# A new order of the parts in the second half of an attention and feed-forward layer, with the moments' two passes apart and turned quarters counted by slot

## The chip, the cores and the metric

The kernel runs on one core of one Trainium2 chip. The metric is the device time of one execution in microseconds (us). Each engine of the core has its own queue of instructions and works through it strictly in order: PE multiplies matrices, DVE and ACT work on vectors, POOL helps them, and SP issues the transfers (DMA). The engines meet only at semaphores: an instruction may wait until a counter has reached a value.

## The reference, cut to what matters

2048 rows x of 2048 numbers pass through a layer in fp32:

```python
h = layernorm(x)
# attention: rat_read -> q, k, v, rope, causal softmax -> attn_out
h = rat_write(h, attn_out)            # gates from attn_out, A = exp(-delta * softplus(...))
g_in, u_in = rat_read(h)              # 4 numbers per head -> 2 x 512, each normalised
mlp_out = silu(g_in @ W0) * (u_in @ W1)        # 512 -> 2048 (ctx_1024 holds W0 and W1)
h = rat_write(h, mlp_out)             # again with 632 outputs from 2048
x = x + h
z = layernorm(x)                      # feed-forward: 8 experts of rank 16
scores = 8 * softmax(z @ Wr + br)
x = x + 2 * sum_e scores_e * (z @ A_e) @ B_e
```

`rat_write` scales the state h (512 heads x 4) by A, adds a term from its second input, and does that by several passes over 2048 numbers per row.

## The kernel before, in words

The rows are cut into 16 tiles of 128 (T = 2048, `NT` = 16) and 4 blocks of 4 tiles. A first half projects q, k and v and does the attention; the change does not touch it. The second half, called the mix, is what the change is about. It begins at about 648 us of the profiled span.

The mix is made of parts. A part is named by a letter, a tile (or block) and a name, as `("a", 5, "gates", None)`:

- a (attention write, tile i): `loado`, `load`, `wod` (16 matmuls into two banks), `low`, `delta`, `gates`, `scale`, `sum`, then four quarters `turn` 0 to 3 (PE transposes 512 columns of the state) and `read` 0 to 3 (PE multiplies a turned quarter), `stats`, `norm`.
- m (the MLP, block b, steps 0 to 63): steps 0 to 31 are "up" steps of 12 matmuls, after which ACT takes a silu and DVE multiplies into `m_hT`; steps 32 to 63 are "down" steps of 8 matmul instructions each. t (block b, k of 8): a quarter of the MLP's input is turned by PE, scaled by DVE into one of two buffers `m_raw`, split by ACT into `m_yhi` and by POOL into `m_ylo`.
- w (MLP write, tile i): `load`, `low`, `delta`, `loadx`, `gates`, `scale`, `sum`, `x` (adds x, DVE, one pass over 2048 numbers).
- e (experts, tile i): `stats` (mean and variance: two ACT passes over 2048 numbers, then POOL), `turn` 0 to 3, `down` 0 to 3, `router`, `weigh`, `lowT`, `out` 0 to 3, `store`. s is one part (16 matmuls) that sums a weight table.

What a part does on an engine stands in `write_pe`, `write_dve`, `write_act`, `expert_pe`, `expert_dve`, `expert_act`, `turn_*` and `mlp_*`. The queue of every engine is made by one walk over one list, `order` (line 1113): every part has a number, its place, and the list is sorted by it. A step of the MLP has the place 64 * block + step, so places are in steps; the other parts stand between steps by a base of their tile plus an offset (tables `A_AT`, `W_AT`, `E_AT`, `FIRST_AT`, `A_BASE`, `W_BASE`, `E_BASE`). Since each engine follows the same list, a part that comes early in it is ahead on all engines.

Most small results go through a ring of two PSUM banks (6 and 7): each `turn`, `low`, `delta`, `lowT`, `out` of an expert and both halves of `wod` from tile 4 on take the next bank of the ring in the list's order, and PE waits until the reader of the bank two claims ago has emptied it. A turned quarter is copied by ACT (`keep_quarter`, line 1573, instruction in line 1577) into one of two slots `m_turned`; a slot is free when the `read` or `down` of the quarter before last has been done. This is counted by one semaphore, `quarter_used`, over all quarters.

Lines of the profile that the prediction speaks of: PE L1262 `turn`, L1277 `wod`, L1292 `delta`, L1320 `down`, L1327 `lowT`, L1332 `out`, L1340 the s part, L1349 t, L1362 up steps, L1374 down steps. DVE L1411 the copy of `wod`'s second bank, L1421 to L1434 `gates`, L1442 to L1452 `scale`, L1455 to L1464 `sum`, L1469 `x`, L1514 `weigh`, L1521 `out`, L1531 t, L1545 the product into `m_hT`. ACT L1577 copy of a quarter, L1611 and L1614 `scale`, L1639 and L1643 the two passes of `stats`, L1664 t, L1676 silu. POOL L1717 t. All transfers are issued in line 141.

## Time and profile before

| what | us |
|---|---|
| median of 3 runs | 1874.23 (1872.31 to 1878.28) |
| the profiled execution's own time | 1873.91 |
| its span | 1872.1 |
| PE busy in the span | 1646.7 (88%) |
| DVE, ACT, POOL busy | 1107.7, 872.0, 272.5 |
| waits of PE longer than 0.25 us between 975 and 1780 us | 78.1 in 42 pieces |

PE is the engine that sets the time; it has work in all stretches. How much it could win is read from three things: its idle time before an instruction and what ended it (in square brackets in a timeline, or summed as waits), its granted clock (PEclk, a share of the full 2.4 GHz, so that a stretch with 0.95 had a tenth of its time at 1.2 GHz), and the same two for the engine that it waited for. Idle time of the other engines costs nothing in itself.

### The profile page before, as it was taken

What the parts mean: (1) busy time and instruction counts of PE and PEld (TensorE: products, weight loads), DVE (VectorE), ACT (ScalarE), POOL (GpSimd) and SP (SyncE); (2) the same over time, 40 slices, a digit from 0 to 9 for tenths busy, and PEclk for the clock granted to TensorE, in tenths of its full rate; (3) what the DMA queues carried; (4) which work ended last, traced back from release to release, by engine and by line L of the source; (5) the groups of instructions that cost most, each with busy time, mean ns of one, the idle gap of its engine ahead of it and who ended that gap; (6) DMA issues with size and microseconds to landing.
All of it is one profiled execution on the core that took longest, in us unless ns stands there. A gap on an engine that the chain in (4) does not pass through costs nothing.

```text
span 1872.1 us, 23561 instructions
## 1 busy us (share of the span) xinstructions
PE 1646.7 (88%) x8854; PEld 1139.9 (61%) x8854; DVE 1107.7 (59%) x1729; ACT 872.0 (47%) x1598; POOL 272.5 (15%) x259
## 2 busy tenths in 40 slices
PE   5799999999999856998989899898998998999966
PEld 4565655666666535776657666556676565776544
DVE  6678755888888566353363744645537443454466
ACT  1333236888877544553243544325445334442243
POOL 0235432434320000200011000003000002000000
PEclk7899999999999975899999999998999999999988
DMA  7366568887864343465556555554655544655621
GB/s 299 115 262 250 201 174 237 224 227 218 227 181 114 124 175 120 161 221 186 182 201 211 176 199 202 164 193 132 225 202 185 184 151 153 212 188 172 234 102 68
DMA packets 117221, 348.69 MB, mean 186 GB/s; under 512 B 16226, under 2 KB 33250, under 8 KB 101876
## 3 DMA queue, kind: packets, MB, share of 16 engines
q1 hardware_dynamic: 117108, 347.19, 57.2%
q8 instruction: 70, 1.15, 0.2%
...
## 4 chain that ended last, share of the span: by engine, by line
PE 61%; DVE 22%; ACT 9%; issue 5%; DMA 1%; POOL 1%; SPq 0%; DVEq 0%; ACTq 0%
PE ps L1362 13%; PE ps L1374 10%; PE ps L395 6%; PE ps L819 4%; PE ps L806 4%; PE ps L1277 4%; PE ps L842 4%; PE ps L1320 3%; PE ps L1305 3%; PE ps L1262 3%; ACT a_p L921 3%; PE ps L1332 2%; DVE m_A L1460 2%; DVE m_A L1456 2%; PE ps L368 2%
## 5 line engine op out<-in xcount | busy, mean ns | idle before, releaser
L1362 PE MATMUL ps<-m_yhi,m_win 128*128 128x512 f32 x1024 | 357.9, 417 | 8.7 <-ACT m_raw L1676 8.7
L1374 PE MATMUL ps<-m_wod,m_hT 128*128 128x512 f32 (+1 forms) x1024 | 303.1, 444 | 8.0 <-DVE m_hT L1545 8.0
L1374 PEld LDWEIGHTS ps<-m_wod,m_hT 128*128 128x128 f32 x1024 | 169.5, 196 | 146.8 <-issue 146.4
L1362 PEld LDWEIGHTS ps<-m_yhi,m_win 128*128 128x128 f32 x1024 | 198.1, 193 | 60.8 <-issue 16.0
L863 DVE TENSOR_REDUCE a_negmax<-ps 128x1 f32<-128x640 f32 (+7 forms) x176 | 180.8, 1027 | 60.5 <-PE ps L809 59.6
L1362 PE MATMUL ps<-m_ylo,m_win 128*128 128x512 f32 x512 | 206.1, 403 | 0.0
L921 ACT ACTIVATE a_p<-ps,a_negmax 128x128 f32<-128x128 f32 (+7 forms) x256 | 188.5, 750 | 28.6 <-DVE a_negmax L863 26.1
L819 PE MATMUL ps<-ident,a_p 128*128 128x128 f32 x1152 | 157.8, 276 | 1.3 <-DVE a_pT L876 1.2
L1545 DVE TENSOR_TENSOR m_hT<-m_raw,ps 128x512 f32<-128x512 f32 x64 | 43.5, 684 | 172.5 <-PE ps L1362 159.6
L1577 ACT ACTIVATE m_turned<-ps 128x512 f32<-128x512 f32 x128 | 74.1, 591 | 152.5 <-PE ps L1262 152.4
L806 PE MATMUL ps<-a_k,a_q 128*128 128x512 f32 (+3 forms) x384 | 124.0, 402 | 16.6 <-ACT a_p L921 14.8
L819 PEld LDWEIGHTS ps<-ident,a_p 128*128 128x128 f32 x1152 | 124.0, 142 | 3.2 <-DVE a_pT L876 1.9
L1362 PEld LDWEIGHTS ps<-m_ylo,m_win 128*128 128x128 f32 x512 | 99.4, 194 | 24.8 <-issue 4.9
L395 PE MATMUL ps<-p_yT,p_wqkv 128*128 128x512 f32 x256 | 112.3, 593 | 0.0
L1262 PE MATMUL ps<-ident,m_hs 128*128 128x128 f32 x464 | 75.5, 296 | 38.8 <-DVE m_hs L1464 14.1
L876 DVE COPY a_pT<-ps 128x512 f32<-128x512 f32 (+3 forms) x190 | 108.1, 576 | 1.3 <-PE ps L819 0.7
L1705 POOL TENSOR_TENSOR m_scale<-m_scale,mhalf 128x2 f32<-128x2 f32 x16 | 12.4, 772 | 634.5 <-DVE m_scale L1482 634.5
L935 ACT ACTIVATE a_pT<-ps 128x512 f32<-128x512 f32 (+3 forms) x154 | 83.9, 545 | 34.8 <-PE ps L819 34.6
L806 PEld LDWEIGHTS ps<-a_k,a_q 128*128 128x128 f32 x384 | 63.3, 192 | 54.8 <-ACT a_p L921 31.5
L1320 PE MATMUL ps<-e_A,m_turned 128*128 128x136 f32 x512 | 76.1, 295 | 21.7 <-ACT m_turned L1577 21.6
L1262 PEld LDWEIGHTS ps<-ident,m_hs 128*128 128x128 f32 x464 | 60.1, 155 | 49.9 <-DVE m_hs L1464 15.3
L1521 DVE TENSOR_TENSOR m_hs<-ps,m_hs 128x512 f32<-128x512 f32 x56 | 38.2, 687 | 88.0 <-PE ps L1332 87.8
...
## 6 DMA issues: line engine op xcount, KB each, us to landing
m_win<-mlp_in_split SPq DMA_DIRECT2D x128, 512.0 KB, 4.2
m_wod<-in_wod2T SPq DMA_DIRECT2D x128, 316.0 KB, 3.1
...
p_xT<-in_xT SPq DMA_DIRECT2D x16, 1024.0 KB, 8.9
p_x<-in_x SPq DMA_DIRECT2D x16, 1024.0 KB, 10.3
...
a_k<-qk_split SPq DMA_DIRECT2D x128, 128.0 KB, 7.3
...
```

Of the source, the lines that this page charges most:

```text
L395: m = nc.tensor.matmul(ps[:, b, :], wq[:, k, col:col + P], yT[:, k, :], start=(ic == 0), stop=(ic == HCH - 1))
L806: nc.tensor.matmul(ps[:, bank + at, c0:c0 + kn], qs[s][:, qt * P:qt * P + P], ks[s][:, k0:k0 + kn], start=True, stop=k0 + kn < klen)
L819: m = nc.tensor.transpose(ps[:, b, P * m_:P * m_ + P], src[:, j, P * k:P * k + P], ident[:, :])
L842: m = nc.tensor.matmul(ps[32 * hh:32 * hh + 32, 6, c0:P * qn], a_v[s][:, k, HD * hh:HD * hh + HD], kept[:, hh, k, c0:P * qn], start=(k == ...
L863: V.tensor_reduce(negmax[:, n % 4, 0:len(units[n][3])], by_head(n, score_banks(n)), AX_X, ALU.max, negate=True).then_inc(max_ready, 1)
L876: V.tensor_copy(kept[:, heads[j0]:heads[j1] + 1, k0:k1 + 1, P * q:P * q + P], ps[:, b, 0:P * len(part)].rearrange("p (a k b) -> p a k b", ...
L921: m = S.activation(dst[:, j, :], src[:, j, :], ACT.Exp, bias=negmax[:, n % 4, j:j + 1], accum_out=rsum[:, si % 2, q * 4 + hh:q * 4 + hh + 1])
L935: S.activation(kept[:, heads[j0]:heads[j1] + 1, k0:k1 + 1, P * q:P * q + P], ps[:, b, 0:P * len(part)].rearrange("p (a k b) -> p a k b", a ...
L1262: m = nc.tensor.transpose(bank_of(what, i, "turn", q)[:, P * j:P * j + P], h[:, P * (4 * q + j):P * (4 * q + j) + P], ident[:, :])
L1320: m = nc.tensor.matmul(bank_of("e", i, "down")[:, 0:EW + NE], tT[quarter["e", i, q] % 2][:, P * (j % 4):P * (j % 4) + P], wA[:, j, :], sta ...
L1362: m = nc.tensor.matmul(bank_of("m", blk, step), win[s][:, wl, ic, :], y[:, k, :], start=(ic == 0 and p3 == 0), stop=(ic == HCH - 1 and p3 ...
L1374: m = nc.tensor.matmul(ps[:, b, 0:cn], hT[:, k, P * q:P * q + P], w2[s][:, c0:c0 + cn], start=(k == 0), stop=(k == MCH - 1))
```

## The change

The tables of places are replaced by one dictionary `PLACES`, with other numbers; the construction of `order` from it is the same. `stats` of the experts becomes two parts: `mean` (first ACT pass and the small scaling, with a new semaphore `emean_ready`) and `spread` (second ACT pass, and POOL). `quarter_used` becomes two semaphores, one for each slot, so that the copy of quarter n waits for the uses of its own slot alone. The instructions are the same in number and kind.

```diff
+PLACES = {'A': {'loado': -2,
+       'wod': 0,
...
+ 'W': {'load': -3.18, 'low': 0, 'delta': 1.6, 'loadx': 2, 'gates': 2.66, 'scale': 3.59, 'sum': 5.81, 'x': 6.93},
...
-        W_AT = [("load", None, -3), ("low", None, 0), ("delta", None, 1.6), ("loadx", None, 2), ("gates", None, 4),
-                ("scale", None, 5), ("sum", None, 6), ("x", None, 8)]
...
-        placed = [(40, ("s", 0, "sum", None))]
+        placed = [(PLACES["s"], ("s", 0, "sum", None))]
...
-        hs_scaled, skip_ready, hs_ready, turnq_mm, quarter_used = (
+        quarter_used = sems("quarter_used", 2)
...
+        emean_ready = sem("emean_ready")
...
+        def wait_for_quarter(e, what, i, q):
+
+            n = quarter[what, i, q]
+            e.wait_ge(quarter_used[n % 2], n // 2 + 1)
...
             n = quarter[what, i, q]
             act.wait_ge(turnq_mm, n + 1)
-            act.wait_ge(quarter_used, n - 1)
+            act.wait_ge(quarter_used[n % 2], n // 2)
...
-            if part == "stats":
-
-                X, m, spare = hs[hs_of["w", i]], e_mv[i % 4], m_x[x_place(i)]
+
+            X, m, spare = hs[hs_of["w", i]], e_mv[i % 4], m_x[x_place(i)]
+            if part == "mean":
                 act.wait_ge(x2_ready, i + 1)
                 act.wait_ge(elw_ready, i - 3)
                 n = act_own.then_inc(S.activation(spare[:, :], X[:, :], ACT.Identity, accum_out=m[:, 0:1]))
                 act.wait_ge(act_own.sem, n)
-                n = act_own.then_inc(S.activation(m[:, 2:3], m[:, 0:1], ACT.Identity, scale=-1.0 / D))
-                act.wait_ge(act_own.sem, n)
+                S.activation(m[:, 2:3], m[:, 0:1], ACT.Identity, scale=-1.0 / D).then_inc(emean_ready, 1)
+            if part == "spread":
+                act.wait_ge(emean_ready, i + 1)
                 S.activation(spare[:, :], X[:, :], ACT.Square, bias=m[:, 2:3],
                              accum_out=m[:, 1:2]).then_inc(evar_ready, 1)
```

The offsets of all parts, before and after, in steps (a part of tile i stands at its base plus this):

| | before | after |
|---|---|---|
| a, tiles 4 to 15: load, gates, scale, sum | 4.2, 6, 7, 8 | 5.27, 7.93, 8.57, 9.57 |
| a: turn 0 to 3 | 12, 12.5, 14, 15 | 13.57, 14.07, 15.57, 16.57 |
| a: read 0 to 3, stats, norm | 13.5, 14.5, 15.5, 16.5, 17.5, 19 | 15.07, 16.07, 17.79, 18.07, 19.07, 20.57 |
| a, tiles 0 to 3: from wod to turn 0, to read 0 | 6, 7 | 6.52, 7.57 |
| w: gates, scale, sum, x | 4, 5, 6, 8 | 2.66, 3.59, 5.81, 6.93 |
| e: stats, or mean and spread | 8.5 | 8.68 and 12.99 |
| e: turn 2, turn 3, down 2, down 3 | 12.5, 13.5, 14, 15 | 14.61, 14.62, 15.47, 15.48 |
| e: out 0 to 3 | 20, 20.5, 21.5, 22 | 19.1, 20.5, 20.51, 22.57 |
| t of block 1, first and last | 55.5, 62.5 | 57.05, 59.87 |
| t of block 2, first and last | 119.5, 126.5 | 120.21, 128.83 |
| t of block 3, first and last | 183.5, 190.5 | 185.58, 191.64 |
| s | 40 | 30.75 |

The bases stay within 0.7 of a step, but for that of tile 2 in w and e (81.01 for 80).

On PE, at the start of the mix, the rows before are the turn of tile 0's first quarter (`m_hs_161`, L1262) and tile 2's `wod` (`m_first_oT_203`, L1277), of which the first matmuls are shown:

```order
L1292 MATMUL ps<-m_duT_144,m_lowT_148 128x512
L1262 MATMUL ps<-ident,m_hs_161 128x128 x4
L1277 MATMUL ps<-m_wod_135,m_first_oT_203 128x512
L1277 MATMUL ps<-m_wod_135,m_first_oT_203 128x120
L1277 MATMUL ps<-m_wod_137,m_first_oT_203 128x512
```

After, with the lines of the changed file (L1361 is `turn`, L1376 `wod`, L1391 `delta`):

```order
L1391 MATMUL ps<-m_duT_144,m_lowT_148 128x512
L1376 MATMUL ps<-m_wod_135,m_first_oT_203 128x512
L1376 MATMUL ps<-m_wod_135,m_first_oT_203 128x120
L1376 MATMUL ps<-m_wod_137,m_first_oT_203 128x512
L1376 MATMUL ps<-m_wod_137,m_first_oT_203 128x120
L1376 MATMUL ps<-m_wod_129,m_first_oT_203 128x512
L1376 MATMUL ps<-m_wod_129,m_first_oT_203 128x120
L1376 MATMUL ps<-m_wod_131,m_first_oT_203 128x512
L1376 MATMUL ps<-m_wod_131,m_first_oT_203 128x120
L1361 MATMUL ps<-ident,m_hs_161 128x128 x8
```

Tile 2's `wod` has moved ahead of tile 0's turns, and two quarters are turned in a row. The same holds for tile 3 and tile 1.

On DVE, at the end of block 0's up steps, the rows before are tile 6's `sum` (`m_hs_161` and `m_A_165`) between the last two products into `m_hT`:

```order
L1545 TENSOR_TENSOR m_hT<-m_raw_188,ps 128x512
L1486 SCALAR_TENSOR_TENSOR m_scale<-m_moments,m_scale 128x2
L1455 TENSOR_TENSOR m_hs_161<-m_hs_161,m_A_165 128x512x3
L1456 SCALAR_TENSOR_TENSOR m_A_165<-m_A_165,m_gate_179 128x1536
L1460 TENSOR_TENSOR m_A_165<-m_A_165,m_att_out 128x1536
L1464 TENSOR_TENSOR m_hs_161<-m_hs_161,m_A_165 128x512x3
L1545 TENSOR_TENSOR m_hT<-m_raw_189,ps 128x512
```

After (L1644 is the product, L1554 to L1563 `sum`, L1541 to L1551 `scale`, L1625 the copy of the s part):

```order
L1541 TENSOR_TENSOR m_tmp_177<-m_delta_175,m_att_ab 128x512
L1545 TENSOR_TENSOR m_tmp_177<-m_tmp_177,m_att_out 128x512
L1551 TENSOR_TENSOR m_hs_161<-m_hs_161,m_tmp_177 128x512
L1625 COPY e_Asum<-ps 128x136
L1644 TENSOR_TENSOR m_hT<-m_raw_189,ps 128x512
L1585 SCALAR_TENSOR_TENSOR m_scale<-m_moments,m_scale 128x2
L1554 TENSOR_TENSOR m_hs_161<-m_hs_161,m_A_165 128x512x3
L1555 SCALAR_TENSOR_TENSOR m_A_165<-m_A_165,m_gate_179 128x1536
```

The last product now stands ahead of the `sum`, and the s part comes just before it.

On ACT, in block 1, the rows before are the two passes of tile 1's `stats` (`m_hs_163`), a silu pair with its table loads, `scale` of tile 9 (`m_hs_161`, `m_A_165`), and the copies of tile 1's turned quarters:

```order
L1639 ACTIVATE m_x,e_moments_153<-m_hs_163 128x2048
L1641 ACTIVATE e_moments_153<-e_moments_153 128x1
L1643 ACTIVATE m_x,e_moments_153<-m_hs_163,e_moments_153 128x2048
L1676 ACT_TABLE_LOAD
L1676 ACTIVATE m_raw_188<-ps 128x512
L1676 ACTIVATE m_raw_189<-ps 128x512
L1678 ACT_TABLE_LOAD
L1611 ACTIVATE m_hs_161<-m_hs_161,nmr_52,rstd_51 128x2048
L1614 ACTIVATE m_A_165<-m_A_165 128x1536
L1577 ACTIVATE m_turned_186<-ps 128x512
L1577 ACTIVATE m_turned_187<-ps 128x512
```

After (L1738 is `mean`, L1743 `spread`, L1776 silu, L1676 the copies, L1710 and L1713 `scale`):

```order
L1738 ACTIVATE m_x,e_moments_153<-m_hs_163 128x2048
L1740 ACTIVATE e_moments_153<-e_moments_153 128x1
L1776 ACT_TABLE_LOAD
L1776 ACTIVATE m_raw_188<-ps 128x512
L1776 ACTIVATE m_raw_189<-ps 128x512
L1778 ACT_TABLE_LOAD
L1676 ACTIVATE m_turned_186<-ps 128x512
L1676 ACTIVATE m_turned_187<-ps 128x512
L1710 ACTIVATE m_hs_161<-m_hs_161,nmr_52,rstd_51 128x2048
L1713 ACTIVATE m_A_165<-m_A_165 128x1536
L1743 ACTIVATE m_x,e_moments_153<-m_hs_163,e_moments_153 128x2048
```

The second pass has moved behind the first two copies, and `scale` of the other tile too.

## Rows read from the trace of the kernel before

**Rows 1.** Part 6 of the page: the loads of x in the mix.

```profile
m_x<-in_x SPq DMA_DIRECT2D x14, 1024.0 KB, 5.5
```

**Rows 2.** Windows: us, PE, PEld, DVE, ACT, POOL busy (x), granted clock, DMA, GB/s.

```profile
975.00:1265.00 290.00, 257.78 (x1172) 181.96 (x1173) 150.77 (x217) 123.10 (x192) 17.49 (x19) 0.95 0.56 187
1265.00:1550.00 285.00, 252.92 (x1153) 179.78 (x1152) 151.28 (x217) 122.48 (x187) 19.93 (x20) 0.95 0.54 181
1550.00:1780.00 230.00, 212.33 (x920) 148.94 (x918) 100.78 (x139) 86.76 (x132) 14.27 (x16) 0.98 0.58 191
```

**Rows 3.** Waits of PE, 975 to 1780 us: us in total, times, longest.

```profile
PE ps L1332 <- DVE m_hs L1521: 22.2, 8, 3.5
PE ps L1320 <- ACT m_turned L1577: 16.1, 6, 2.8
PE ps L1262 <- ACT m_turned L1577: 11.1, 3, 3.9
PE ps L1349 <- DVE m_raw L1531: 10.5, 5, 4.9
PE ps L1362 <- ACT m_raw L1676: 8.7, 6, 2.1
PE ps L1277 <- ACT e_lowT L1655: 4.0, 7, 0.6
PE ps L1262 <- DVE m_hs L1469: 3.2, 3, 2.2
```

**Rows 4.** Timeline of PE at tile 0's first turn.

```profile
676.38 1.12 PE L1262 MATMUL ps<-ident,m_hs 128*128 128x128 f32 x4 [5.86 <-DVE m_hs L1464]
677.28 6.11 PE L1277 MATMUL ps<-m_wod,m_first_oT 128*128 128x512 f32 x16
```

**Rows 5.** Waits of DVE, 648 to 750 us, as rows 3.

```profile
DVE m_mlp_ab L1411 <- PE ps L1277: 20.0, 4, 12.4
DVE m_hs L1452 <- ACT m_hs L1611: 8.0, 3, 3.7
```

**Rows 6.** Timeline around block 0's first down step, and the s part.

```profile
885.78 1.19 PE L1374 MATMUL ps<-m_wod,m_hT 128*128 128x512 f32 x1 [7.97 <-DVE m_hT L1545]
...
915.22 3.88 PE L1340 MATMUL ps<-e_A,e_weighted 128*128 128x136 f32 x32
```

**Rows 7.** Groups of DVE: count, busy us, mean ns, idle before.

```profile
L1464 DVE TENSOR_TENSOR m_hs<-m_hs,m_A 128x1536 f32<-128x1536 f32 x26 | 45.7, 1758 | 0.9
```

**Rows 8.** Timeline of tile 1's third `out`, and the window behind it, as rows 2.

```profile
1111.06 2.07 PE L1332 MATMUL ps<-e_B,e_lowT 128*128 128x512 f32 x2 [2.77 <-DVE m_hs L1521]
...
1111.00:1116.40 5.40, 5.34 (x15) 3.66 (x16) 3.23 (x7) 2.65 (x5) 0.20 (x1) 0.72 0.06 22
```

**Rows 9.** Timeline: the second pass of tile 1's `stats`, and its first `down`.

```profile
1053.60 2.01 ACT L1643 ACTIVATE m_x<-m_hs,e_moments 128x2048 f32<-128x2048 f32 x1
...
1063.40 2.18 PE L1320 MATMUL ps<-e_A,m_turned 128*128 128x136 f32 x8 [2.61 <-ACT m_turned L1577]
```

**Rows 10.** POOL's line 1717 (ns: shortest, median, longest), and a timeline in block 1.

```profile
L1717 POOL TENSOR_TENSOR m_ylo<-m_raw,m_yhi x32: 1255/1274/3722, 752.9 to 1579.2; 128x512 fp32r<-128x512 f32 x32
...
982.37 3.72 POOL L1717 TENSOR_TENSOR m_ylo<-m_raw,m_yhi 128x512 fp32r<-128x512 f32 x1 [2.87 <-ACT m_yhi L1664]
...
984.99 2.72 DVE L1460 TENSOR_TENSOR m_A<-m_A,m_att_out 128x1536 f32<-128x1536 f32 x1
```

**Rows 11.** The chain of waits: one up step, from its start, with its us.

```profile
1141.46 2.81 PE ps L1362 x12
```

**Rows 12.** Timeline of the end; its second row is four down steps.

```profile
1759.31 0.69 DVE L1521 TENSOR_TENSOR m_hs<-ps,m_hs 128x512 f32<-128x512 f32 x1 [5.88 <-PE ps L1332]
...
1766.01 8.81 PE L1374 MATMUL ps<-m_wod,m_hT 128*128 128x512 f32 x32
...
1782.75 1.97 PE L1262 MATMUL ps<-ident,m_hs 128*128 128x128 f32 x8 [7.93 <-DVE m_hs L1469]
...
1830.95 0.48 PE L1327 MATMUL ps<-ident,e_weighted 128*128 128x128 f32 x1 [16.79 <-DVE e_weighted L1514]
```

More of the change, by code:

```diff
@@ L1079, in program @@
         CONSTS_SET, LOWS_SET, ONES_SET = ZEROS + 8, ZEROS + 12, ZEROS + 13
-        A_AT = [("loado", None, -2), ("wod", None, 0), ("low", None, 2), ("delta", None, 4), ("load", None, 4.2),
-                ("gates", None, 6), ("scale", None, 7), ("sum", None, 8), ("turn", 0, 12), ("turn", 1, 12.5),
-                ("read", 0, 13.5), ("turn", 2, 14), ("read", 1, 14.5), ("turn", 3, 15), ("read", 2, 15.5),
-                ("read", 3, 16.5), ("stats", None, 17.5), ("norm", None, 19)]
-        W_AT = [("load", None, -3), ("low", None, 0), ("delta", None, 1.6), ("loadx", None, 2), ("gates", None, 4),
-                ("scale", None, 5), ("sum", None, 6), ("x", None, 8)]
@@ L1091, in program @@
-        E_AT = [("stats", None, 8.5), ("turn", 0, 10), ("turn", 1, 10.5), ("down", 0, 12), ("turn", 2, 12.5),
-                ("down", 1, 13), ("turn", 3, 13.5), ("down", 2, 14), ("down", 3, 15), ("router", None, 16),
-                ("weigh", None, 17.2), ("lowT", None, 18.5), ("out", 0, 20), ("out", 1, 20.5), ("out", 2, 21.5),
-                ("out", 3, 22), ("store", None, 23)]
-        FIRST_AT = [("loado", None, -100), ("load", None, -99.9), ("wod", None, 0), ("low", None, 1),
-                    ("delta", None, 2), ("gates", None, 3), ("scale", None, 4), ("sum", None, 5), ("turn", 0, 6),
-                    ("turn", 1, 6.5), ("read", 0, 7), ("turn", 2, 7), ("read", 1, 7.5), ("turn", 3, 7.5),
-                    ("read", 2, 8), ("read", 3, 8.5), ("stats", None, 9), ("norm", None, 10)]
@@ L1106, in program @@
         for i in range(NT):
[L1107 to L1112 removed]
+            for what, table, base in (("a", "FIRST" if i < TB else "A", "a"), ("w", "W", "w"), ("e", "E", "e")):
+                for part, at in PLACES[table].items():
+                    q = int(part[-1]) if part[-1].isdigit() else None
+                    placed.append((PLACES[base][i] + at, (what, i, part.rstrip("0123"), q)))
@@ L1307, in write_pe @@
                                          read2[:, jj, :, :].rearrange("p b c -> p (b c)"), start=True, stop=True)
-                m.then_inc(quarter_used, 1)
+                m.then_inc(quarter_used[quarter[what, i, q] % 2], 1)
         def expert_pe(i, part, q):
@@ L1322, in expert_pe @@
                                          start=(j == 0), stop=(j == DCH - 1))
-                m.then_inc(quarter_used, 1)
+                m.then_inc(quarter_used[quarter["e", i, q] % 2], 1)
             if part == "lowT":
@@ L1473, in write_dve @@
                     yv = bank_of(what, i, "read", a).rearrange("p (j o h) -> p j o h", o=RD2, h=HPC)
-                    dve.wait_ge(quarter_used, quarter[what, i, 2 * a + 1] + 1)
+                    wait_for_quarter(dve, what, i, 2 * a + 1)
                     for o in range(RD2):
@@ L1492, in expert_dve @@
             if part == "router":
-                dve.wait_ge(quarter_used, quarter["e", i, 3] + 1)
+                wait_for_quarter(dve, "e", i, 3)
                 dve.wait_ge(evar_ready, i + 1)
@@ L1707, in expert_pool @@
         def expert_pool(i, part, q):
-            if part == "stats":
+            if part == "spread":
                 m = e_mv[i % 4]
```

119 lines of the change are left out of this document (107 added, 12 removed).

## The prediction

> **What bounds the kernel now.** I read the page first: PE is busy in 88% of the span. Then the windows of the mix: in the two long stretches from 975 to 1265 and from 1265 to 1550 us PE is busy 258 of 290 and 253 of 285 us, at a mean granted clock of 0.95 [rows 2]. So PE bounds them, and what can be won is what it stands still and what it does at 1.2 instead of 2.4 GHz. Last I read who ended PE's waits. From 975 to 1780 us seven groups of them make 75.8 us [rows 3], and they repeat with each tile, since each tile's parts stand at the same offsets. The reader is to see there that no engine is full: DVE is busy 151 of 290 us [rows 2], and PE waits for it because of what stands ahead in DVE's queue, not because of how much there is. The same goes for ACT. A new order can therefore pay, with not one instruction less.
>
> **The change part by part.** Durations are of the profiled execution, which took 1873.9 us (span 1872.1); the median of the three runs is 1874.2, so the two can be taken as one.
>
> (a) Tiles 0 to 3. PE waits 5.86 us for tile 0's `sum` and only then does tile 2's `wod`, 6.11 us [rows 4]; DVE in turn waits for that `wod`. After the change `wod` stands ahead of the turn, so it fills PE's wait. DVE's waits for `wod` in this stretch are 20.0 us, of which 12.4 are the very first and stay: 7.6 go. DVE also waits 8.0 us for ACT's scaled state [rows 5]; ACT does that pass after three copies of quarters and in future after two, and it starts sooner because the copies do: I take 5 of 8.0. The bounds are nothing, if ACT becomes what DVE waits for, and 7.6 + 8.0 = 15.6; I take 12.6, nearer to the upper one, since DVE's waits for `wod` are sure to go. The weights of the earlier `wod` are loaded two tiles ahead in SP's queue, and the store of the state that SP issues at the turn now stands behind them, which helps them.
>
> (b) The end of block 0's up steps. PE waits 7.97 us for the last product [rows 6], which DVE does after tile 6's `sum`; four passes of 1.76 us stand ahead of it [rows 7], 7.0 us. They move behind it, and about 1 us is left. The s part, 3.88 us of PE [rows 6], goes from step 40 to just ahead of this place; it fills part of what would remain in any case, so it isn't counted. With 1 us of clock that such a wait costs: 8 us. Bounds: 0 and 7.97 + 3.88 = 11.9.
>
> (c) The turned quarters of the MLP's input (t) and the experts' first turns between them. PE waits 10.5 us for DVE's `m_raw` and 11.1 us for ACT's copies [rows 3], in three blocks. The cause is a second moments pass of 2.01 us [rows 9] and the `scale` and `sum` of another tile between them. In the new order the mean stands before the first t, the spread behind most, and in block 1 all eight t come before tile 8's `sum`; in block 2 the `sum` of tile 12 still stands before the fifth t. I lay out what is left as 2 to 3 us per block, 7 in all: 14.6 us won. Bounds 0 and 21.6.
>
> (d) The tile cycles of blocks 1 to 3. `out` 2 waits 22.2 us in eight places [rows 3] because its ring bank is that of `out` 1, and DVE adds `out` 1 after the `gates` and the `stats` of two other tiles. `gates` now stand before or right behind `out` 0, and `out` 1 and 2 come together, on the bank before: these waits go. `down` 0 waits 16.1 us and the silu pairs make PE wait 8.7 us; both stand behind the two passes of `stats`, and the one pass of 2.01 us that moves [rows 9], together with `x` standing one step earlier, is enough for waits of at most 2.8 and 2.1 us [rows 3]. The wait for `x` at the experts' first turn (3.2) goes too, since `gates` of w stand 1.3 steps earlier. Sum 22.2 + 16.1 + 8.7 + 3.2 = 50.2. What comes in its place: `wod` waits 4.0 us in seven places now, for one ACT copy [rows 3]. In the new order it follows `lowT` and, in tiles 10 and perhaps 14, `w` `delta` at once on PE; it then waits for ACT's copy of a quarter, then for two passes over `delta`: I set 2.7 us, just under the longest ACT wait of its kind, 2.8. With 0.9 in the five others that is 9.9, so 6 more. `out` 0 and 1, and `low` behind them, can wait fractions of a microsecond: for these and for what I do not see I set 12 tile cycles at 0.6, the size of the small waits in rows 3: 7. Won: 50.2 - 6 - 7 = 37. Bounds: 0 and 50.2.
>
> The SP queue: `load` of a stands 1.1 steps later, `x` 1.1 steps earlier with `loadx` where it was. Five steps lie between `loadx` and `x`, of 8.81 / 4 = 2.2 us at least [rows 12], 11 us; the transfer takes 5.5 [rows 1]. That hides it; if it didn't, DVE would wait at each of 16 `x`. The two `quarter_used` semaphores only loosen a wait, and the split of `stats` adds one wait on ACT for its own earlier instruction: nothing.
>
> (e) The clock. After a wait of 2.77 us the granted clock was 0.72 in the next 5.4 us [rows 8], that is 0.28 x 5.4 = 1.5 us lost. Over the stretches 0.05 x 290, 0.05 x 285 and 0.02 x 230 make 33 us [rows 2], an upper bound, since time in which PE stands still is in it. Seven long `out` waits, six `down` waits and some four of (c) times 1.5 are 25. The new waits of (d) take some of that back, about a third: I take 16. Bounds 0 and 25.
>
> (f) The end. The first turn of tile 12 waits 7.93 us for `x` [rows 12]; DVE's `gates` of w 12 stand behind `out` 0 of tile 11, for which DVE waits 5.88 us [rows 12]. `gates` move ahead of it: 5 us. The wait of 16.79 us [rows 12] stays, since DVE is busy there from one end to the other with `gates`, `scale` and `sum` of tiles 14 and 15, and with the same passes after the change. The last tile's first copies come one pass of 2 us sooner, and `x` of tile 15 a little: 3. Won 8; bounds 0 and 13.
>
> Sum: 12.6 + 8 + 14.6 + 37 + 16 + 8 = 96.2; 1873.9 - 96.2 = 1777.7, so 1778. All upper bounds together: 15.6 + 11.9 + 21.6 + 50.2 + 25 + 13 = 137.3, 1737.
>
> **A rule weighed.** POOL's `m_ylo` passes take 1.27 us in the median, but up to 3.72 beside a pass of DVE's `sum`, which itself takes 2.72 instead of 1.76 [rows 7, 10]. The Trainium skill ("SBUF — State Buffer", section "SBUF: two separate sides") says that DVE and GpSimd take turns on a shared pair of ports, which is "an exclusive lock, not a bandwidth split": a DVE pass with two SBUF inputs shuts a GpSimd one out. This case's trace agrees with that place; by the rule the closer t of block 1, with `gates` and `scale` of tile 8 between them, would be slow ones. What that would make of the time is the second rival.
>
> **The rivals.**
> 1. The waits move instead of going: with one in-order queue per engine, what no longer stands ahead of `out` stands ahead of something else. For it: the new gaps that I find already (`wod` behind `delta`, t 5 of block 2 behind a `sum`). Against it: DVE and ACT have half of their time free [rows 2]. It halves (c), (d) and (e): 1778 + (14.6 + 37 + 16)/2 = 1812.
> 2. POOL paces the t of blocks 1 and 3. Eight passes at 3.72 are 29.8 us [rows 10]; PE has some three down steps of 2.2 us and 5 us of turns and `down` between the first and last t of block 1, 12 in all, and six steps and 5 us, 18, in block 3 [rows 12]. It would wait 18 + 12 = 30 more: 1808. Against it: half of all 32 passes took at most 1.27.
> 3. Slower than before: `x` of w now follows its `sum` almost at once, and `sum` comes before the `norm` of a, the last product of a pair and, in two tiles, `out` 3. If PE needs one of these before DVE is through, it waits for four passes, 7.0 us [rows 7], and 1.5 for the clock [rows 8], in each of 12 cycles: 12 x 8.5 = 102, so 1778 + 102 = 1880. It decides against the change from a mean wait of 6.5 us per cycle on. Against it: PE does four up steps of 2.81 us, 11 us, until it needs the bank of a product [rows 11].
> 4. The order changes but the time does not: something that the waits hide, such as the weights' transfers, sets the pace. Then 1874. Against it: in rows 3 no wait of PE was ended by a transfer.
>
> **How the numbers follow.** The forecast, 1778, gets 0.63 (its own range 1756 to 1800); rival 1, at 1812, 0.20; rival 2, at 1808, 0.08; rival 3, 0.05; rival 4, 0.04. The range for 8 times in 10: below, not quite all upper bounds, 1748; above, rival 1 with another quarter of its waits kept, 1836. A change of 0.3% (5.6 us) is what a measurement of this kernel tells from none: faster 0.91, the same 0.04, slower 0.05.
>
> **What would show it.** In the profile after, L1332's wait for DVE and L1320's for ACT are near nothing in blocks 1 to 3; the down steps of block 0 start with at most 1 to 2 us of wait; the stretch of tiles 0 to 3 is some 12 us shorter; the clock in blocks 1 and 2 is 0.98; `wod` has its longest wait in tile 10; the 16.8 us before tile 13's `lowT` are still there. I am wrong if the waits of PE between blocks 1 and 3 sum to over 45 us, if the t have 3 us each, or if `x` waits for a transfer.

## The result, and the profile after

The changed kernel takes 1761.84 us, median of four runs (1759.10 to 1764.08), against 1874.98 us (1872.31 to 1878.28) for the kernel before on the same chip: a ratio of 0.9395, 95% interval 0.9373 to 0.9417, or 113 us less. I had forecast 1778 with a range of 1748 to 1836. The profiled execution took 1764.08 us (span 1762.3).

Every line number of PE's, DVE's and ACT's code is 99 higher than before: L1361 is `turn`, L1376 `wod`, L1419 `down`, L1426 `lowT`, L1431 `out`, L1448 t, L1461 and L1473 up and down steps; on DVE L1554 to L1563 `sum`, L1568 `x`, L1620 `out`, L1630 t; on ACT L1676 the copy of a quarter, L1710 `scale`, L1723 `norm`, L1738 and L1743 `mean` and `spread`. First the windows, columns as in [rows 2], whose three stretches now lie here:

```profile
946.00:1205.00 259.00, 248.09 (x1176) 176.51 (x1174) 158.35 (x220) 123.02 (x193) 34.48 (x20) 0.99 0.60 205
1205.00:1462.00 257.00, 248.61 (x1168) 177.70 (x1169) 155.48 (x218) 121.92 (x188) 32.09 (x20) 0.98 0.62 208
1462.00:1670.00 208.00, 206.13 (x926) 145.87 (x924) 96.94 (x139) 88.16 (x136) 13.09 (x16) 1.00 0.61 199
```

PE is now busy in 248 of 259, 249 of 257 and 206 of 208 us, and at nearly full clock. Its busy time fell too, with the same number of instructions. The whole mix in one window shows how much, before and after:

```profile
648.00:1870.00 1222.00, 1058.56 (x4752) 750.88 (x4752) 620.14 (x881) 506.08 (x784) 79.31 (x80) 0.93 0.53 178
```

```profile
648.00:1870.00 1222.00, 1034.17 (x4752) 737.46 (x4752) 623.39 (x881) 502.89 (x784) 105.34 (x80) 0.96 0.53 179
```

The same 4752 instructions of PE take 1058.6 us before and 1034.2 after: 24.4 us less. Most of it is the clock: of PE's busy time in the mix 122.2 us lie in stretches granted 1.2 GHz before and 81.3 after, and half of the difference, 20.5 us, is what the clock gave back, by an estimate that takes all of PE's work as twice as fast at 2.4 GHz. The other 4 us were not traced. The rest is time in which PE stood still: its waits of 0.2 us and more in the mix, added up from the timeline, are 164.8 us before and 79.3 after, 85.5 less. 24.4 and 85.5 make the 110 us by which the profiled executions differ. The waits of PE from 946 to 1670 us, to be read beside [rows 3]:

```profile
PE ps L1448 <- ACT m_y L1723: 5.1, 2, 3.7
PE ps L1361 <- DVE m_raw L1630: 3.8, 1, 3.8
PE ps L1448 <- DVE m_raw L1630: 2.7, 2, 2.3
PE ps L1376 <- ACT m_turned L1676: 2.0, 2, 1.1
PE ps L1376 <- ACT e_lowT L1755: 1.5, 2, 0.9
PE ps L1376 <- ACT m_delta L1691: 1.4, 1, 1.4
PE ps L1361 <- ACT m_att_out L1686: 1.4, 2, 0.7
PE ps L1376 <- DVE m_hs L1620: 1.0, 1, 1.0
```

The waits for `out` (22.2 us), for the first `down` (16.1) and for the silu pairs (8.7) are not there any more. What is new is small but for two waits of 3.7 and 3.8 us: t of block 2 waits for tile 11's `norm`, and a turn behind it for a t that stands behind tile 12's `sum`.

### The profile page after: what moved, and what is told of

The parts are those of the page before. It is cut to its first block, busy times and chain, and to the rows that moved or that the text cites. A ratio compares the mean times of both kernels' runs of the same rounds, so it can differ in the third digit from the quotient of the medians.

```text
span 1762.3 us, 23558 instructions
## 1 busy us (share of the span) xinstructions
PE 1624.5 (92%) x8854; PEld 1128.2 (64%) x8854; DVE 1111.1 (63%) x1729; ACT 868.9 (49%) x1598; POOL 298.6 (17%) x259
## 3 DMA queue, kind: packets, MB, share of 16 engines
q1 hardware_dynamic: 117108, 347.19, 60.8%
## 4 chain that ended last, share of the span: by engine, by line
PE 75%; DVE 13%; ACT 6%; issue 3%; DMA 1%; POOL 1%; SPq 0%; DVEq 0%; ACTq 0%
PE ps L1461 20%; PE ps L1473 13%; PE ps L509 6%; PE ps L933 5%; PE ps L920 4%; PE ps L956 4%; PE ps L1376 4%; PE ps L1419 3%; PE ps L1361 3%; PE ps L1404 3%; PE ps L1431 3%; ACT a_p L1035 3%; PE ps L482 2%; PE ps L1391 1%; PE ps L495 1%
## 5 line engine op out<-in xcount | busy, mean ns | idle before, releaser
L1461 PE MATMUL ps<-m_yhi,m_win 128*128 128x512 f32 x1024 | 349.0, 409 | 0.0
L1473 PE MATMUL ps<-m_wod,m_hT 128*128 128x512 f32 (+1 forms) x1024 | 298.0, 440 | 1.3 <-DVE m_hT L1644 0.9
L1473 PEld LDWEIGHTS ps<-m_wod,m_hT 128*128 128x128 f32 x1024 | 166.7, 194 | 136.6 <-issue 136.5
L1461 PEld LDWEIGHTS ps<-m_yhi,m_win 128*128 128x128 f32 x1024 | 193.6, 189 | 47.8 <-issue 4.1
L1461 PE MATMUL ps<-m_ylo,m_win 128*128 128x512 f32 x512 | 202.9, 396 | 0.0
L1644 DVE TENSOR_TENSOR m_hT<-m_raw,ps 128x512 f32<-128x512 f32 x64 | 43.7, 684 | 172.9 <-PE ps L1461 164.8
L1676 ACT ACTIVATE m_turned<-ps 128x512 f32<-128x512 f32 x128 | 72.7, 593 | 146.9 <-PE ps L1361 139.8
L1805 POOL TENSOR_TENSOR m_scale<-m_scale,mhalf 128x2 f32<-128x2 f32 x16 | 21.7, 1358 | 534.9 <-DVE m_scale L1581 534.9
L1461 PEld LDWEIGHTS ps<-m_ylo,m_win 128*128 128x128 f32 x512 | 97.0, 189 | 23.7 <-issue 4.1
L1049 ACT ACTIVATE a_pT<-ps 128x512 f32<-128x512 f32 (+3 forms) x154 | 83.9, 545 | 34.1 <-PE ps L933 34.0
L920 PEld LDWEIGHTS ps<-a_k,a_q 128*128 128x128 f32 x384 | 63.4, 192 | 55.1 <-ACT a_p L1035 32.0
L509 PEld LDWEIGHTS ps<-p_yT,p_wqkv 128*128 128x128 f32 x256 | 47.6, 190 | 55.0 <-issue 55.0
L1361 PE MATMUL ps<-ident,m_hs 128*128 128x128 f32 x464 | 68.7, 284 | 13.1 <-DVE m_raw L1630 3.8
L482 PEld LDWEIGHTS ps<-p_read,p_xT 128*128 128x128 f32 x512 | 68.0, 215 | 19.0 <-issue 19.0
L669 ACT ACTIVATE p_y<-p_z,p_yscale 128x512 f32<-128x512 f32 x48 | 35.6, 804 | 89.9 <-DVE p_yscale L588 89.9
```

Source lines behind the costliest of these rows:

```text
L482: m = nc.tensor.matmul(ps[:, j // 4, zw * (j % 4):zw * (j % 4) + zw], p_xT[i % 2][:, j, :], read1[:, j, :, :].rearrange("p a b -> p (a b)" ...
L509: m = nc.tensor.matmul(ps[:, b, :], wq[:, k, col:col + P], yT[:, k, :], start=(ic == 0), stop=(ic == HCH - 1))
L920: nc.tensor.matmul(ps[:, bank + at, c0:c0 + kn], qs[s][:, qt * P:qt * P + P], ks[s][:, k0:k0 + kn], start=True, stop=k0 + kn < klen)
L1049: S.activation(kept[:, heads[j0]:heads[j1] + 1, k0:k1 + 1, P * q:P * q + P], ps[:, b, 0:P * len(part)].rearrange("p (a k b) -> p a k b", a ...
L1361: m = nc.tensor.transpose(bank_of(what, i, "turn", q)[:, P * j:P * j + P], h[:, P * (4 * q + j):P * (4 * q + j) + P], ident[:, :])
L1461: m = nc.tensor.matmul(bank_of("m", blk, step), win[s][:, wl, ic, :], y[:, k, :], start=(ic == 0 and p3 == 0), stop=(ic == HCH - 1 and p3 ...
```

## The experiments

Each kernel has the changed code and differs from the changed kernel (1761.8), or from the kernel of experiment 1, in places alone. All ratios are to the kernel before, which was run again beside each set of experiments (medians of 1874.5 to 1876.2 us), with their 95% intervals. A difference to 1761.8, which comes from another set, can be off by a microsecond or two for that reason.

**1. The code without the places.**

```diff
-'W': {'load': -3.18, ..., 'gates': 2.66, 'scale': 3.59, 'sum': 5.81, 'x': 6.93},
+'W': {'load': -3, ..., 'gates': 4, 'scale': 5, 'sum': 6, 'x': 8},
...
+# A, E, FIRST, the bases, t and s as before as well; spread directly behind mean
```

> The changed code with the places of the kernel before (spread directly behind mean, so each engine has its instructions in the old order). My theory: all of the gain is the order; the two semaphores and the split of stats cost and give nothing, so 1874 within 0.3% (1868 to 1880), and PE's longest waits stand at the old places (7.97 before the first down step, 16.79 before tile 13's lowT). Rival: counting the quarters by slot alone loosens ACT's copies, of whose waits PE had 11.1 us at the turns; then it is 1865 or less.

1875.95 us, ratio 1.0003 (0.9994 to 1.0013). In the old order the two semaphores and the split give nothing, so the gain needs the new places. Whether the new order would do as well with one semaphore for all quarters was not tried.

**2. Tiles 0 to 3 put back.**

```diff
-'FIRST': {..., 'wod': 2.06, 'low': 3.06, ..., 'turn0': 8.58, 'turn1': 8.59, 'turn2': 9.2, ...}
+'FIRST': {..., 'wod': 0, 'low': 1, ..., 'turn0': 6, 'turn1': 6.5, 'turn2': 7, ...}
```

> The changed kernel, but tiles 0 to 3 have the offsets of the kernel before, nothing else. The stretch up to the first t was 103.5 us before and 89.1 after. My theory (term a): all 14.4 of it come back and nothing else moves: 1776, the waits before the first turns of tiles 0 and 1 are back at 5.9 and 4.3 us. Rival: what is lost here is given back later, since block 0's up steps have slack in their other engines: under 1770.

1780.24 us (0.9493, 0.9476 to 0.951), 18.4 more than the change. In the trace the stretch before the first t is 106.2 us long, and everything behind it takes as long as in the changed kernel to within 1 us. That is four more than I expected, and the pair of profiles that I had worked from is why. Seven profiled kernels have the new order of this stretch (the change and experiments 3, 4 and 8 to 11): it takes 83.5, 83.7, 85.4, 85.4, 85.6, 89.1 and 89.2 us, and the 89.1 is the change. Six have the old order: 103.5 to 106.2 us, and the 103.5 of the kernel before is the low end. The means, 105.2 and 86.0, differ by 19.2, which agrees with the 18.4.

**3. The outs put back, with `gates` and `scale` of w.**

```diff
-'W': {..., 'gates': 2.66, 'scale': 3.59, ...}   'E': {..., 'out0': 19.1, 'out1': 20.5, 'out2': 20.51, 'out3': 22.57, ...}
+'W': {..., 'gates': 4, 'scale': 5, ...}         'E': {..., 'out0': 20, 'out1': 20.5, 'out2': 21.5, 'out3': 22, ...}
```

> The changed kernel, but the four outs stand at 20, 20.5, 21.5 and 22 again, and gates and scale of w at 4 and 5. My theory (term d, its out part, and e): the waits of the third out come back, eight of 2.8 to 3.5 us or 22 us of waits, and each of them with 1.5 us of clock: 34 more, 1796; the granted clock from block 1 on goes from 0.99 to 0.97. Rival 1 (waits only move): with the other waits gone DVE's queue has more slack, the out waits that come back are matched by shorter others, and it is under 1774.

1791.68 us (0.9556, 0.9534 to 0.9579): 29.8 more, near the 34 that I expected, but not by the waits that I expected. The edit puts two things back at once, the outs and `gates` and `scale` of w, so that 29.8 is not the price of either. DVE and PE in block 1:

```profile
1138.30 0.68 DVE L1620 TENSOR_TENSOR m_hs<-ps,m_hs 128x512 f32<-128x512 f32 x1
...
1140.73 1.75 DVE L1554 TENSOR_TENSOR m_hs<-m_hs,m_A 128x1536 f32<-128x1536 f32 x1
...
1145.97 1.76 DVE L1563 TENSOR_TENSOR m_hs<-m_hs,m_A 128x1536 f32<-128x1536 f32 x1
1147.65 0.68 DVE L1620 TENSOR_TENSOR m_hs<-ps,m_hs 128x512 f32<-128x512 f32 x1
```

```profile
1148.39 1.22 PE L1431 MATMUL ps<-e_B,e_lowT 128*128 128x512 f32 x1 [6.08 <-DVE m_hs L1620]
```

The third `out` now stands behind another tile's whole `sum` on DVE, since its base had moved as well, and the fourth waits 6.08 us. That is the one long wait before an `out`; another, of 6.53, stands before tile 12's `delta`, the first t of block 3 waits 5.88 instead of 1.37, and the turns at the end wait longer too. Putting back one part of a fitted order can make waits that neither kernel has.

**4. The second moments pass put back.**

```diff
-'E': {'mean': 8.68, ..., 'spread': 12.99, ...}
+'E': {'mean': 8.68, ..., 'spread': 8.69, ...}
```

> The changed kernel, but spread stands directly behind mean (8.69 instead of 12.99). Three answers. As the prediction has it, the pass that moves is what frees the first down (16.1 us of waits) and the silu pairs (8.7), with some nine long waits and 1.5 us of clock each: up to 38 more, 1800. If the earlier x is what does it, the second pass is done before the copies are wanted, and it is within 4 us: under 1766. If both are needed, each first down waits about half of its 2.6 us, too short for the clock to fall, and t of blocks 1 to 3 some 2 us more: 12 more, 1774. I hold the last for likeliest.

1762.57 us (0.9399, 0.9381 to 0.9417): no difference from the change, where I had held 12 us more for likeliest. The new part `spread`, on which my terms for `down` and t rested in part, gains nothing that this measurement can tell. In the trace the turns of blocks 1 and 3 wait 1.4 and 2.0 us for ACT's copies again (3.4 us instead of 0.8), but no `down` of blocks 1 to 3 stands among the waits, and from the first up step on the profiles take 1016.8 and 1016.4 us.

**5 and 6. From the kernel before: `x` alone, then the row of w.**

```diff
 # 5
-'W': {..., 'gates': 4, 'scale': 5, 'sum': 6, 'x': 8}
+'W': {..., 'gates': 4, 'scale': 5, 'sum': 6, 'x': 6.93}
 # 6
-'W': {..., 'gates': 4, 'scale': 5, 'sum': 6, 'x': 8}
+'W': {..., 'gates': 2.66, 'scale': 3.59, 'sum': 5.81, 'x': 6.93}
```

> The places of the kernel before in the changed code, with one number changed: x of w stands at 6.93 instead of 8. DVE then adds x directly behind sum, ahead of the last product of a pair. The run with only spread put back lost nothing, so x may be what freed the first down and the silu pairs. Theory 1, x alone does it: the waits for m_turned at the first down (16.1 us), for m_raw at the silu pairs (8.7) and at the experts' first turn (3.2) go, with some nine falls of the clock of 1.0 to 1.5 us each: 1876 less 28 less 9 is 1839. Theory 2, as the prediction had it, x and the moved pass are needed together: half of the waits and little clock, 1860. Theory 3: DVE is busy there anyway and the product that is now behind x makes PE wait: 1872 or more. I hold the first for likeliest, with 1845.

> The places of the kernel before in the changed code, with the whole row of w as in the change: gates 2.66, scale 3.59, sum 5.81, x 6.93; a, e, t, s and tiles 0 to 3 are as before. gates then stand ahead of the first out. Theory 1: that removes the third out's waits too (22.2 us, with eight falls of the clock of 1.5), on top of what x gives: 1839 less 34 is 1805, 60 to 70% of the whole gain from one row of four numbers. Theory 2 (waits move): gates ahead of out 0 make it wait for out 0 instead and the moments of a still stand between out 0 and 1, so half of it: 1822 or more.

`x` alone: 1871.57 us (0.9976, 0.9967 to 0.9985), 4 us, where I had held 1845 for likeliest. In its trace DVE has `x` of this tile done 9.9 us after it begins the third `out`, against 10.4 in the kernel before: the new place is ahead of one product of 0.68 us and of nothing else. The row of w: 1796.32 us (0.9584, 0.9568 to 0.96), 79.5 us or seven tenths of the whole gain, from four numbers; I had expected 1805. ACT in the `x` kernel, ahead of tile 1's first `down` (lines one lower here: L1775 is silu, L1709 and L1712 `scale`, L1675 the copies):

```profile
1060.17 2.01 ACT L1742 ACTIVATE m_x<-m_hs,e_moments 128x2048 f32<-128x2048 f32 x1
...
1063.58 1.09 ACT L1775 ACTIVATE m_raw<-ps 128x512 f32<-128x512 f32 x2
1064.68 1.28 ACT L1777 ACT_TABLE_LOAD   x1
1065.97 2.10 ACT L1709 ACTIVATE m_hs<-m_hs,nmr,rstd 128x2048 f32<-128x2048 f32 x1
1067.98 1.47 ACT L1712 ACTIVATE m_A<-m_A 128x1536 f32<-128x1536 f32 x1
1069.35 1.06 ACT L1675 ACTIVATE m_turned<-ps 128x512 f32<-128x512 f32 x2
```

This is the cause of the 16.1 us in [rows 3], and I had it wrong: the copies that `down` waits for stand behind the second pass only at several removes; directly ahead of them is `scale` of tile 9, which follows a silu pair, which follows the passes, and the first pass waits for DVE's `x` (6.15 us in this trace). As long as DVE hands over `x` late, the whole chain is late. The kernel with the row of w has the same order on ACT, and the copies' waits there are 6.1 us instead of 16.1 (next experiment).

**7. `gates` alone.**

```diff
-'W': {..., 'gates': 4, ...}
+'W': {..., 'gates': 2.66, ...}
```

> The places of the kernel before in the changed code, with one number changed: gates of w stands at 2.66 instead of 4, so its six instructions are ahead of the first out on DVE. The run with the whole row of w was 79 us faster than before, that with x alone 4. My theory: gates is what does it, since without it the third out waits for nothing and sum comes earlier by the same 3 us: 1796 plus the 4 that x gave, 1800. Rival: scale and sum moved with it (5 to 3.59, 6 to 5.81) carry a good part, and it is 1820 or more.

1833.76 us (0.9778, 0.9757 to 0.9799), 41 us; I expected 75. Waits of PE from 975 to 1700 us:

```profile
PE ps L1418 <- ACT m_turned L1675: 16.1, 6, 2.8
PE ps L1360 <- ACT m_turned L1675: 11.2, 3, 3.9
PE ps L1447 <- DVE m_raw L1629: 10.3, 5, 4.9
PE ps L1460 <- ACT m_raw L1775: 8.4, 6, 2.0
```

The waits for `out` are gone, those for `down` and silu stand as in [rows 3]. With the row of w the same view reads:

```profile
PE ps L1360 <- ACT m_turned L1675: 10.6, 3, 3.9
PE ps L1418 <- ACT m_turned L1675: 6.1, 6, 1.1
PE ps L1375 <- ACT e_lowT L1754: 4.0, 7, 0.6
PE ps L1447 <- DVE m_raw L1629: 3.8, 2, 2.1
PE ps L1447 <- DVE m_hs L1619: 3.0, 2, 2.4
```

So `gates` frees `out`, and the other three numbers, on top of it, free the silu pairs and most of `down`. `x` was worth 4 by itself and some 38 are won by `scale`, `sum` and `x` on top of `gates`; how these 38 divide among the three, and what they give without `gates`, was not tried.

**8. t put back.**

```diff
-'t': [..., 57.05, 57.45, 57.85, 58.26, 58.66, 59.06, 59.47, 59.87, ...]
+'t': [..., 55.5, 56.5, 57.5, 58.5, 59.5, 60.5, 61.5, 62.5, ...]
```

> The changed kernel with the t of blocks 1 to 3 at their old places (55.5, 56.5 and so on). Theory (term c): 10.4 us of waits return, with three or four falls of the clock of 1.5: 1762 and 15 is 1777. Rival: the waits at t came from the moments pass and from x, which now stand elsewhere, so the old places cost under 5 us: 1767 or less.

1783.69 us (0.9507, 0.9491 to 0.9524): 21.9 more, where I expected 15. In its trace PE waits 7.74 us for a t behind tile 8's `sum`, 5.85 and 5.70 for `norm` before the first t of blocks 2 and 3, and 4.56 for the last t of block 2.

**9. The end of block 0's up steps put back.**

```diff
-'s': 30.75
+'s': 40, and tile 6's sum at 30.9
```

> The changed kernel, but tile 6's sum again stands ahead of block 0's last product (at 30.9 instead of 31.57), and s at 40. Theory (term b): the 7.1 us of waiting before the first down step come back, with 1 to 3 us of clock: 1771. Rival: what DVE does late here it gives back in the down steps that follow, or s at its new place mattered by itself: outside 1767 to 1775.

1772.17 us (0.9454, 0.944 to 0.9468): 10.3 more, within the range expected. In its trace the wait before the first down step is 9.90 us, against 0.87 in the change and 7.97 before, so that 9.0 of the 10.3 are the wait.

**10. Three parts alone, in the kernel before.**

```diff
+the row of w, the offsets of tiles 0 to 3, s at 30.75 and tile 6's sum behind the last product
 # all else, t and the outs and the offsets of a included, as before
```

> The places of the kernel before with three parts of the change alone: the row of w, the offsets of tiles 0 to 3, and tile 6's sum behind block 0's last product (with s at 30.75). Theory, the parts add up: 1796.3 - 18.4 - 10.3 = 1767.6, within 6 us of the whole change (1762), although putting t back in the whole change cost 22 and putting the outs back cost 30, since those places only fit each other. Rival: they don't add up, because the t and out places of the change are needed for the gain of the others; then it is 1775 or more.

1767.47 us (0.943, 0.9411 to 0.9449), where the sum of the parts gave 1767.6. These three make 107 of the 113 us. What is then missing, t and the outs with the offsets of a, the bases and `spread`, adds only 6 us, although putting back t alone cost 22: the old places of t do harm only among the new places of the others. The 30 of experiment 3 cannot be set beside these 6, since it took back `gates` and `scale` of w too, which this kernel has.

**11 and 12. The waits that are left.**

```diff
+('a', 11, 'norm'): 118.9, ('a', 15, 'norm'): 182.9      # ahead of x
+('a', 12, 'sum'): 126.38, ('a', 8, 'gates'): 59.1       # behind the sixth t
+('w', 14, 'low'): 255.475, ('w', 14, 'delta'): 256.02, ('w', 15, 'low'): 256.5
+('e', 12, 'lowT'): 258.45, ('e', 13, 'weigh'): 261.7, ('e', 13, 'lowT'): 262.0
+('e', 13, 'turn', 1): 256.03, ('e', 13, 'out', 1 to 3): 265.0 to 265.02, ('e', 15, 'mean'): 270.7
 # 12 has this and
+'s': -0.6
```

> The changed kernel with other places for its remaining waits: norm of tiles 11 and 15 ahead of x (waits of 3.69 and 1.37 us before t of blocks 2 and 3), sum of tile 12 behind the sixth t instead of the fifth's product (3.77), gates of tile 8 behind the sixth t (2.25), and in the end: low and delta of tile 14 right behind the last down step, tile 12's lowT ahead of the second moments pass, tile 13's weigh ahead of tile 14's sum, three of tile 13's outs behind tile 15's x on DVE, tile 15's mean behind two copies. Theory: 3 + 1.4 + 3.8 + 2.2 us of waits in the blocks, with 1.5 us of clock for three of them, and 5 in the end: 20 less, 1742. Rival (waits move): each of these parts now makes something else wait, sum of tile 12 its own turn and the last down step's copy above all, and it is within 5 us of the change: 1757 or more.

> The version with the other places for the remaining waits (1744.8), with the s part moved from step 30.75 to just ahead of block 0's first t, where PE waits 3.85 us for the last norm of the first tiles. s takes 3.9 us at full clock. Where it stands now the clock is full; at its new place the granted clock is 0.50, so that it takes some 7.7 us, of which 3.85 lie in the wait: 3.9 saved in block 0 and 3.9 lost here, 1745, if the clock there stays at 0.50 up to the first up step as before. If the clock follows what PE does, it is granted full sooner, and s and the t behind it (8.1 us of PE at 0.50) win: up to 4 from the t and 2 from s, 1739. I hold 1741 for likeliest: the clock rises with the filler before the t are through. Over 1748 would say that s delays DVE's first products of the t.

The first gives 1744.78 us (0.9298, 0.9277 to 0.9319), 17 us less than the change, near the 20 expected, and the lowest median here. In its trace the 3.69 us before t of block 2 are 0.77, the 3.77 before a turn 0.47, and tile 13's `lowT` waits 5.13 us instead of 12.61, though tile 14's turns and first `down` now wait 6.9 us (the four below) where 2.9 stood:

```profile
1699.73 0.48 PE L1443 MATMUL ps<-ident,e_weighted 128*128 128x128 f32 x1 [5.13 <-DVE e_weighted L1630]
...
1709.45 1.10 PE L1378 MATMUL ps<-ident,m_hs 128*128 128x128 f32 x8 [2.73 <-DVE m_hs L1585]
1712.21 3.99 PE L1436 MATMUL ps<-e_A,m_turned 128*128 128x136 f32 x16 [1.66 <-ACT m_turned L1693]
1716.98 1.11 PE L1378 MATMUL ps<-ident,m_hs 128*128 128x128 f32 x4 [0.78 <-DVE m_last_hs L1637]
1719.78 1.11 PE L1378 MATMUL ps<-ident,m_hs 128*128 128x128 f32 x4 [1.69 <-DVE m_last_hs L1637]
```

With s in front of the first t it is 1747.99 us (five runs, 0.9322, 0.9308 to 0.9335): the same within the intervals, where I had held 1741 for likeliest. The wait there is filled, but s itself, which I had priced at half clock, ran at full:

```profile
730.47 3.97 PE L1456 MATMUL ps<-e_A,e_weighted 128*128 128x136 f32 x32 [1.17 <-DMA e_A<-in_expA]
```

PE starts it when its weights land, 1.17 us into the wait. From the end of s to the first up step it is then 9.4 us; without s it was 13.8 from the start of the wait, of which 3.85 were the wait, so the t themselves won only half a microsecond. What ate at least part of the gain is at the end of the up steps, where s had covered a wait for the last product: 0.87 us before, 2.98 now.

## Why the prediction was right, and where it was not

The mechanism was right: PE sets the time, the gain is waits that one in-order queue made for another, and with them clock. The sum was 96 where 110 came (profiled executions). The waits were forecast at 80 and measured at 85.5, PE's shorter work at 16 and measured at 24.4. The terms that were mis-sized are (d), 9 too low, and (e), 8 too low; (c) and (f) were 4 and 3 too high. That the sum came out nearer than its terms is in part luck. By its steps:

**(a), 12.6 forecast.** The stretch went from 103.5 to 89.1 us, 14.4, and putting it back cost 18.4. Its make-up on DVE was off: DVE's waits for `wod` fell by 4.1 instead of 7.6, those for ACT's `scale` by 6.6 instead of 5 ([rows 5] beside these, DVE, 648 to 735 us). What I had seen in [rows 4] came true: tile 2's `wod` now stands ahead of tile 0's turn, with no wait between (the second fence):

```profile
DVE m_mlp_ab L1510 <- PE ps L1376: 15.9, 2, 12.0
...
DVE m_hs L1551 <- ACT m_hs L1710: 1.4, 2, 1.0
```

```profile
673.14 6.08 PE L1376 MATMUL ps<-m_wod,m_first_oT 128*128 128x512 f32 x16
679.06 1.04 PE L1361 MATMUL ps<-ident,m_hs 128*128 128x128 f32 x8
```

In this pair of profiles the gain is all waits (PE's fell from 39.5 to 25.7 us, its busy time only from 64.1 to 63.4). Over the six and seven profiles of experiment 2 the waits fall by 12.7 us in the mean, which is the term, and PE's busy time by 6.5. The term held no clock, and six of these 6.5 are clock: half of the fall in PE's busy time at 1.2 GHz, from 41.8 to 29.7 us.

**(b), 8.** The wait of 7.97 us is 0.87, 7.1 less; experiment 9 measured 10.3, more than the wait that the kernel before had:

```profile
867.85 2.39 PE L1473 MATMUL ps<-m_wod,m_hT 128*128 128x512 f32 x8 [0.87 <-DVE m_hT L1644]
```

**(c), 14.6.** The lines for t and the turns beside it make 13.2 us after (5.1, 3.8, 2.7 and two of 0.8), against 21.6 in [rows 3], 1.3 for a `norm` and 1.0 for turns behind a t: 10.7 won. The part missed is `norm` of tiles 11 and 15, which is behind `sum` and `x` of w on DVE; I had laid out t against `sum` and not against `norm`:

```profile
1206.15 1.12 PE L1448 MATMUL ps<-ident,m_y 128*128 128x128 f32 x4 [3.69 <-ACT m_y L1723]
...
1231.90 1.33 PE L1361 MATMUL ps<-ident,m_hs 128*128 128x128 f32 x6 [3.77 <-DVE m_raw L1630]
```

The second is the fifth t of block 2 behind tile 12's `sum`, as forecast. Experiment 11 takes both away.

**(d), 37.** 54.2 us of waits (these four groups and `wod`) became 7.9: 46.3. `wod` waits 5.9 where I had set 9.9, and what I did not see is 2.0 where I had set 7; its longest wait is in tile 10, 1.4 instead of 2.7. The term was too low by 9, and one step had the wrong cause: `x` alone does not free `down` (experiment 5), and the moved pass is not needed for it (experiment 4). `gates` of w ahead of the first `out` frees the outs and leaves the 16.1 us of `down` as they were; `scale`, `sum` and `x` moved as well bring them to 6.1 (experiments 6 and 7), and the last 6.1 go with other places of the change, which ones was not tried. For the pass to matter, ACT would have to be late because of it; ACT was late because DVE was.

**(e), 16.** 24.4 us less of PE's busy time, 20.5 of them by the estimate from the clock. They were won where I had looked for them: between block 0's first up step and tile 12's first turn PE's busy time at 1.2 GHz fell from 61.7 to 15.0 us, worth 23, near the bound of 25; in tiles 0 to 3 it stayed (39.1 and 39.3), and at the end it rose. I had let the new waits take a third back. Between 946 and 1670 us they are 1.4 us and less but for three, and behind a wait of that size the clock did not fall; it did behind the longer ones. Windows of the changed kernel behind the wait of 1.38 us, around that of 2.25 and behind that of 3.69, and last of experiment 4's kernel around the same wait as the second:

```profile
1055.00:1062.00 7.00, 6.32 (x29) 4.27 (x30) 0.28 (x1) 2.79 (x7) 0.00 (x0) 1.00 0.47 158
959.40:966.20 6.80, 6.77 (x28) 4.58 (x29) 6.29 (x7) 5.60 (x6) 3.75 (x3) 0.75 0.12 20
1205.40:1212.20 6.80, 6.05 (x17) 3.98 (x18) 0.81 (x1) 3.88 (x7) 1.28 (x1) 0.50 0.97 355
...
956.70:963.50 6.80, 6.69 (x35) 4.54 (x36) 6.29 (x7) 5.54 (x6) 3.68 (x3) 1.00 0.33 102
```

The granted clock is 1.00, 0.75 and 0.50, and 1.00 in the last: a wait of 2.24 us that the clock followed in one kernel's execution and not in the other's. The length of a wait alone does not settle it, so a fixed 1.5 us for each wait could only be near. One profile sizes this term loosely as well: the kernel of experiment 4, as fast as the change, has 14 us less of PE's busy time in the mix and 9 us more of waits. In the sum of the waits (d)'s 9 more and (c)'s 4 less nearly cancel.

**(f), 8.** From the wait before tile 12's first turn to the end it is 92.2 us before (1774.8 to 1867.0) and 86.9 after (1670.3 to 1757.1): 5.3. The turn's wait went from 7.93 to 2.57, as forecast. The wait before tile 13's `lowT` is 12.61, not 16.8, but a new one of 4.03 stands before tile 12's first `out`, whose copy on ACT is behind the second moments pass of tile 13. PE's waits there fell by 8.3 us (34.1 to 25.8), but its own work took 3 us more (57.9 to 60.8 us) for the same number of instructions. The mean clock of the stretch, 0.83 and 0.84, hides why: it counts the time in which PE stands still. Of PE's busy time 13.5 us lie at 1.2 GHz before and 18.9 after, worth 2.7 us.

```profile
1672.82 1.78 PE L1361 MATMUL ps<-ident,m_hs 128*128 128x128 f32 x8 [2.57 <-DVE m_hs L1568]
...
1699.34 1.12 PE L1431 MATMUL ps<-e_B,e_lowT 128*128 128x512 f32 x2 [4.03 <-ACT e_lowT L1755]
...
1721.23 0.48 PE L1426 MATMUL ps<-ident,e_weighted 128*128 128x128 f32 x1 [12.61 <-DVE e_weighted L1613]
```

**The rivals.** Rival 1, that waits move: in the changed kernel few did, but it is what happened in experiments 3 and 8; in 2, 4 and 9 it did not. Rival 2, that POOL paces the t: its passes did become slow, up to 4.44 us against 3.72 in [rows 10], and PE waited for none of them directly.

```profile
L1817 POOL TENSOR_TENSOR m_ylo<-m_raw,m_yhi x32: 1264/1276/4442, 738.7 to 1488.3; 128x512 fp32r<-128x512 f32 x32
```

```profile
965.85 7.19 POOL L1817 TENSOR_TENSOR m_ylo<-m_raw,m_yhi 128x512 fp32r<-128x512 f32 x2 [2.34 <-ACT m_yhi L1764]
```

The slow pair, 4.44 and 2.78 us, lies beside tile 8's `sum` on DVE, two of whose passes take 2.71 us instead of 1.74. The ends alternate: POOL's first pass ends at 970.29 us, DVE's third of `sum` at 971.91, POOL's second at 973.03, DVE's fourth at 974.65, each 1.1 us (POOL) or 1.6 us (DVE) behind the other engine's, a little less than a pass of usual length takes (1.27 and 1.74), as if they took turns. That agrees with the rule weighed in the prediction (the Trainium skill, "SBUF — State Buffer", section "SBUF: two separate sides"). But the up steps that read `m_ylo` begin at 974.3, 1.2 us after the last pass, so it is hidden. I had priced it as if PE waited for each pass; only the last before the first up step counts. What PE does feel of POOL comes by way of DVE. Tile 8's `gates` has a pass of 2.88 us that begins together with a POOL pass of 1.27, where such a pass takes 1.76 in the kernel before; behind it stands the t for which PE waits 2.25 us, so about half of that wait is POOL's:

```profile
954.81 1.27 POOL L1817 TENSOR_TENSOR m_ylo<-m_raw,m_yhi 128x512 fp32r<-128x512 f32 x1 [1.32 <-ACT m_yhi L1764]
...
954.82 2.88 DVE L1528 TENSOR_TENSOR m_A<-m_delta,m_gate 128x1536 f32<-128x1536 f32 x1
```

Rivals 3 and 4 found nothing: in blocks 1 to 3 no wait for `x` is left, and none was ended by a transfer.
